# A two-layer attention and expert block: attention normalised in four pieces between pairs of score maxima, its output projection one slot later, and GpSimd's residual sum behind a layer norm

## The reference

```python
x = x + _L0_xattn_ref(_layernorm(x, axis=-1), ctx_768, ...)   # 16 heads of 8
x = x + _L0_ffn_ref(_layernorm(x, axis=-1), ...)              # squared relu; routed part
x = x + _L1_xattn_ref(_layernorm(x, axis=-1), ctx_768, ctx_768, ...)  # one head of 128
x = x + _L1_ffn_ref(_layernorm(x, axis=-1), ...)              # 8 experts, each takes its top tokens
```

```python
attn = jnp.einsum('bhqd,bhkd->bhqk', q, k) * scale
attn = jax.nn.softmax(attn, axis=-1)
x = jnp.einsum('bhqk,bhkd->bqhd', attn, v).reshape(B, Nq, Cq)
return x @ Wo + bo
```

## Time and profile before

| | before |
|---|---|
| median of 3 runs | 264.07 us (263.54 to 264.34) |
| the profiled execution, its own time | 264.77 us |
| its span in the profile | 262.7 us |
| PE busy | 210.8 us, 80% |
| DVE busy | 155.9 us, 59% |
| ACT, POOL busy | 87.5 us (33%), 83.7 us (32%) |
| chain that ended last, by engine | DVE 34%, PE 34%, POOL 11% |
| reciprocals L1260, 5 of them | 13.5 us |
| score maxima L1239, 64 of them | 27.4 us |

### The profile page before, as it was taken

One profiled execution on the slowest core, in us unless ns is written; L12 is line 12 of the kernel. 1 busy time (PEld: TensorE's weight loads), 2 busy tenths in 40 slices (PEclk: granted clock), 3 DMA queues, 4 the chain that ended last, 5 costly groups with the idle time before them and its releaser, 6 DMA issues.

```text
span 262.7 us, 3477 instructions
## 1 busy us (share of the span) xinstructions
PE 210.8 (80%) x1203; PEld 122.6 (47%) x1212; DVE 155.9 (59%) x523; ACT 87.5 (33%) x183; POOL 83.7 (32%) x91
## 2 busy tenths in 40 slices
PE   1797589998799969989999988998897998676400
PEld 0543245335364545366635554653333796666400
DVE  5898837619859989386739665768899122011100
ACT  3241046352433543155402323226710355050200
POOL 1348507000106011101110321300006678885454
PEclk9999999999999999999999999999999999797955
DMA  7600111001100007931100101200001223332222
GB/s 203 176 9 23 45 47 50 20 2 50 30 1 4 0 0 243 331 109 45 41 0 5 40 0 41 85 13 31 0 2 32 53 27 46 43 42 31 24 24 20
DMA packets 15190, 13.04 MB, mean 50 GB/s; under 512 B 3520, under 2 KB 12161, under 8 KB 15169
## 3 DMA queue, kind: packets, MB, share of 16 engines
q1 hardware_dynamic: 11440, 10.17, 12.5%
q0 software_dynamic: 3008, 2.31, 6.5%
q10 hardware_dynamic: 721, 0.30, 0.4%
HBM read 7.99 MB, written 3.21 MB: 43 GB/s over the span
## 4 chain that ended last, share of the span: by engine, by line
DVE 34%; PE 34%; POOL 11%; issue 7%; DMA 6%; ACT 3%; another core or an unknown queue 2%; POOLq 1%; DVEq 0%; ACTq 0%
PE psum L884 7%; POOL out L1632 6%; DVE rden L1260 5%; DVE mrow L1239 5%; DVE xn L1192 4%; PE psum L802 4%; DMA out<-pT,idx 3%; DVE stats L1183 3%; DVE pT L1401 2%; POOL pT L1623 2%; DMA pT<-gather_rows,idx 2%; PE psum L807 2%; PE psum L866 2%; POOL rstd L1563 2%; PE psum L840 2%
## 5 line engine op out<-in xcount | busy, mean ns | idle before, releaser
L802 PE MATMUL psum<-c 128*128 128x512 bf16 x183 | 44.7, 379 | 0.5
L699 ACT ACTIVATE pT<-psum 103x512 f32<-103x512 f32 (+1 forms) x48 | 28.4, 597 | 45.0 <-PE psum L868 44.9
L1562 POOL TENSOR_SCALAR ve<-mv 128x4 f32<-128x4 f32 (+1 forms) x19 | 4.3, 229 | 95.3 <-DVE mv L1186 95.2
L1239 DVE TENSOR_REDUCE mrow<-psum 128x4 bf16<-128x308 f32 x64 | 27.4, 470 | 5.1 <-PE psum L840 4.6
L1632 POOL DMA_INDIRECT out<-pT,idx x16 | 25.4, 1586 | 14.2 <-DMA out<-pT,idx 5.8
L1623 POOL DMA_INDIRECT pT<-gather_rows,idx x16 | 16.7, 1044 | 31.7 <-DVE idx L1461 27.1
L802 PEld LDWEIGHTS psum<-c 128*128 128x128 bf16 x192 | 18.4, 99 | 17.4 <-issue 0.6
L1469 DVE TENSOR_TENSOR pT<-psum,b_rows 128x256 f32<-128x256 f32 x8 | 3.4, 425 | 34.3 <-PE psum L1143 24.1
L840 PE MATMUL psum<-k_stack,q_stack 128*128 128x308 f16 x64 | 16.7, 298 | 7.2 <-DVE mrow L1239 6.8
L773 ACT ACTIVATE pT<-psum,b 128x256 f32<-128x256 f32 x32 | 13.6, 474 | 18.5 <-PE psum L1128 18.5
L1143 PE MATMUL psum<-w,pT 128*128 128x128 f32 x128 | 19.0, 309 | 0.8 <-ACT pT L773 0.8
(11 more groups left out here) (179 smaller groups left out, 352.8 us busy)
## 6 DMA issues: line engine op xcount, KB each, us to landing
w<-in_L_ffn_W SPq DMA_DIRECT2D x16, 256.0 KB, 5.9
gather_rows<-xrow SPq DMA_DIRECT2D x4, 272.0 KB, 2.1
x<-in_x SPq DMA_DIRECT2D x4, 256.0 KB, 4.4
out<-res SPq DMA_DIRECT2D x4, 256.0 KB, 2.0
q_stack<-q_hi SPq DMA_DIRECT2D x24, 32.0 KB, 1.8
q_stack<-q_lo SPq DMA_DIRECT2D x24, 32.0 KB, 1.9
b_rows<-in_L_ffn_b SPq DMA_DIRECT2D x1, 512.0 KB, 3.9
pT<-gather_rows,idx POOLq DMA_INDIRECT x16
```

The costliest lines, as they stand in the source:

```text
L699: nc.scalar.activation(pT[0:n, b % 2, s, :], ST_ps[s % 2][0:n, :], ACT.Exp).then_inc(exp_done, 1)
L802: pe.matmul(bank[b][:, :], ident16, c16[:, 0:4 * P], start=True, stop=True)
L1239: dve.tensor_reduce(mrow[:, b % 2, j, g * GH:(g + 1) * GH], S_ps[u % 2][:, 0:GK].rearrange("p (h k) -> p h k", h=GH), X, ALU.max).then_inc ...
```

## The change

Sequences 0, 1 and 2 are normalised in four quarters of 128 columns, each a reciprocal and a product: two in slot 2, one in slot 4 and one in slot 5 (each behind the score maxima of its slot). The projection on PE and the residual sum on DVE move from slot 5 to slot 6 for these sequences. The last sequence is left as it was. POOL waits, ahead of the residual start and the key stack of sequence 3, until DVE has applied the third layer norm of sequence 0.

```diff
--- before.py
+++ after.py
@@ -974,7 +974,7 @@
                         pe.transpose(tail2_ps[:, 0:E * FC], b1_rows[:], ident[0:E * FC, 0:E * FC]).then_inc(b1_ps_done, 1)
                     for u, j0, j1, ps, _ in units(t) if 0 <= t < B else ():
                         cols = slice(j0 * P, j1 * P)
-                        if s == 5:
+                        if s == (6 if t < B - 1 else 5):
                             pe.wait_ge(attT_done, u + 1)
                             if t == 0:
                                 pe.wait_ge(ld_q, 48)
@@ -1253,12 +1253,14 @@
                                             value_mask[0:CW, c, :].unsqueeze(1).broadcast_to([CW, G, GD]), ALU.mult)
                 ins.then_inc(v8_done, 1)
 
-            def normalise(b):
-                dve.wait_ge(o_ps_done, b + 1)
-                for _, j0, j1, _, _ in units(b):
-                    cols = slice(j0 * P, j1 * P)
-                    settle(dve.reciprocal(rden[:, cols], den_ps[:, cols]))
-                    dve.tensor_tensor(attT[:, cols], O_ps[:, cols], rden[:, cols], ALU.mult).then_inc(attT_done, 1)
+            def normalise(b, j0, j1):
+                if j0 == 0:
+                    dve.wait_ge(o_ps_done, b + 1)
+                cols = slice(j0 * P, j1 * P)
+                settle(dve.reciprocal(rden[:, cols], den_ps[:, cols]))
+                ins = dve.tensor_tensor(attT[:, cols], O_ps[:, cols], rden[:, cols], ALU.mult)
+                if j1 in [end for _, _, end, _, _ in units(b)]:
+                    ins.then_inc(attT_done, 1)
 
             with nc.allow_low_precision("a shift of the exponent that numerator and denominator share"):
                 dve.memset(half_neg[:], -0.5).then_inc(half_set, 1)
@@ -1364,12 +1366,17 @@
                                 settle(dve.tensor_reduce(den1[:, t % 2, js], p1[:, js], X, ALU.add))
                                 dve.reciprocal(r1[:, t % 2, js], den1[:, t % 2, js]).then_inc(r1_done, 1)
                         t = ph - 1
-                        if 0 <= t < B and s == 2:
-                            normalise(t)
+                        if t == B - 1 and s == 2:
+                            for _, j0, j1, _, _ in units(t):
+                                normalise(t, j0, j1)
+                        if 0 <= t < B - 1 and s in (2, 4, 5):
+                            normalise(t, s - 2, s - 1)
+                            if s == 2:
+                                normalise(t, 1, 2)
                         for u, j0, j1, ps, _ in units(t) if 0 <= t < B else ():
                             added = ps[1][:, :].rearrange("p (j d) -> p j d", j=J)[:, j0:j1]
                             stream = rtiles(t)[:, j0:j1]
-                            if s == 5:
+                            if s == (6 if t < B - 1 else 5):
                                 dve.wait_ge(wo_ps_done, u + 1)
                                 dve.wait_ge(res0_done, t + 1)
                                 settle(dve.tensor_tensor(stream, added, stream, ALU.add))
@@ -1599,6 +1606,8 @@
             residual(0)
             for ph in range(B + 2):
                 if ph + 1 < B:
+                    if ph >= 2:
+                        pool.wait_ge(xn_done[2], ph - 1)
                     residual(ph + 1)
                     if ph >= 1:
                         stack_keys(ph + 1)
```

## The result

The changed kernel takes 279.69 us (median of 4 runs, 276.32 to 281.24) against 263.92 for the kernel before (median of 4): ratio 1.0555, 95% interval 1.0457 to 1.0652. The forecast was 272.2 with a range to 275.5. The direction was right and the size too small by almost half. The ratio and its interval compare the means of the fast runs alone (278.6 of three of these four against 263.9), and the run of 281.24 counts as slow.

The account below looks back on a forecast made before the run. DVE's own order was taken to bound phases 1 to 3, with PE waiting. 2.70 + 2.55 + 2.89 = +8.14 on the profiled 264.77 gave 272.9, or 272.2 on the median; range 268.0 to 275.5, own range 270.5 to 274.

Parts of the forecast that it names:

- Bound of the phases: Phases 1 to 3: DVE's own order sets the end, PE waits, and delayed transposes reach the end in full.
- Part 1: Normalisation on DVE: a quarter takes 1.20 us, 0.27 of it fixed; 0.81 more per sequence, 2.4 in all.
- Parts 2 and 3: Maxima between quarters, projection and sum in slot 6: DVE idles; with the pieces' cost, phases +2.70, +2.55, +2.89 us.
- Part 4: POOL's wait around 80 us: applies get 2.9 us back, but only 0.3 reaches the chain, since PE's sums end later.
- rival 3: TensorE's clock falls after PE's waits in slots 6 to 8, once or twice: 273.8 to 275.4 us; chance 0.12.

Follow-up runs that it names:

- the quarters alone: Kernel before with four quarters back to back in slot 2 for sequences 0 to 2, nothing else changed: 266.47 us, ratio 1.0089.
- With the clock held: Changed kernel plus matmuls that nobody reads in PE's waits ahead of the scores of slots 6 and 8, the projection and the transposes: 273.55 us, ratio 1.0355.
- the second trace: Profile of the unmodified changed kernel measured again on one chip beside others: median 279.72 us, ratio 1.0571; the traced execution took 279.61.
- the move alone: Kernel before with only projection and residual sum moved to slot 6 for sequences 0 to 2: 269.34 us, in two groups, ratio 1.0153 for the first.
- all four kernels here: Fillers added to the changed kernel (273.55 us), the projection and sum move (267.74), 384 and 128 column pieces (267.82), and early sequence 0 normalisation with further edits (261.88).

## Why the prediction was wrong

- **Bound of the phases: right.** DVE's order sets them. The idle stretches ahead of the maxima, of L1361 and of the third projection are in the trace with their releasers, within 0.1 us of the forecast; those ahead of the first two residual sums are longer (0.78 and 0.48 for 0.34).
- **Part 1, the pieces: right.** 1.19 a quarter for 1.20 (the reciprocal alone 0.95, where 0.85 was named); the quarters alone cost 2.6 for 2.4.
- **Parts 2 and 3, the order: right in kind, a little small.** With the clock held, the changed kernel is 9.7 above the kernel before, against 8.14. The traces have 0.3 a phase: maxima and `v` take 1.46 when DVE has just idled ahead of them instead of 1.28, the projection to the sum 1.19 (1.49 where the clock fell) instead of 1.16, apply to transposes 1.17 instead of 1.07. I took these steps from rows in which DVE was never idle, where part of each lay beside its neighbour. The last 0.7 of the 9.7 lies outside the phases, which add up to 9.0: the two profiled executions are 8.9 apart (273.63 and 264.77). The prediction took 0.7 off its sum since that execution of the kernel before was so much above its median; the profiled one with PE kept busy is only 0.1 above its own.
- **Part 4, GpSimd's wait: right.** 0.2 us in the trace for 0.3, and no gain that the times can tell.
- **The step that failed is TensorE's clock.** The sum has it at nothing, and rival 3 gave it 0.12 and "1.6 more for a fall", once or twice. Holding the clock gives 6.2 us back (279.7 to 273.6), and the sign that the prediction itself had named, a granted clock below 1.00 between 60 and 130 us, is in both traces of the changed kernel. The chance was too low: it came from one window that had stood it (1.98 us busy of 4), while the change puts such stretches into every phase, and the two traced executions met two and three falls. The price was right only for a short fall: one of 1.6 us is in the second trace too, but others kept the clock low for two to four times as long and cost 3.1, 4.1 and, in the kernel with the move alone, 5.2 us. Rival 3 and the forecast should have been one case.
- How the 15.8 us come about, by runs: quarters 2.6, move 3.7, the clock 6.2. The 3.4 that are left of the 9.7 are a remainder and no run's own measurement: they go with the quarters standing between the maxima, and with whatever quarters and move cost only together.

What stays open: what decides in which of the waits the clock falls, and how long it stays low. In the first trace of the changed kernel a wait of 2.60 us in phase 3 passed without a fall; in the second the clock was down behind it:

```profile
129.43 1.16 PE L982 MATMUL psum<-w_q,attT 128*128 128x128 f32 x8 [2.60 <-DVE attT L1261]
...
135.28 0.66 PE L807 MATMUL psum<-c,xn 128*128 128x128 f32 x4 [0.80 <-DVE xn L1192]
```

## What to carry to other kernels

Where DVE's own order is the path, cutting one of its instructions into pieces to let others in costs the fixed part of each piece, and it pays only if what is let in is ready. Ask for each inserted step when its input comes: here the scores came no sooner, and the steps that used to hide the projection and GpSimd's power had been moved away from beside them. When a change adds waits of TensorE of a microsecond or more to a dense stretch, count the clock into the forecast itself, and test it by filling the waits with matmuls that nobody reads: in all four kernels here that brought the median down, by 1.6 to 6.2 us, and the executions to within 1.8 us of each other.

## What the runs showed of the hardware

- TensorE's granted clock fell to the lower of its levels behind waits close together, the longest of them 1.05 to 2.60 us in the traces, and stayed there for 3 to 14 us (an estimate from the windows' granted clocks), which cost 0.3 to 5.2 us. Ahead of one fall PE was busy for 1.20 us of 4 (the move alone, 68 to 72); in the changed kernel's first trace 1.62 of 4 (92 to 96) and a wait of 2.60 us passed at full clock. Two executions of the same kernel had two falls and three, one of them at the same place.
- DVE's reciprocal from PSUM took 0.95, 1.75, 2.56 and 3.35 us for 128, 256, 384 and 512 columns: 0.8 us for each 128 and 0.15 fixed.
- Four `tensor_scalar` of 128x128 from SBUF to SBUF took 3.9 us beside GpSimd's two `tensor_tensor`, and 1.1 when GpSimd came after them. A reciprocal that reads PSUM took the same beside GpSimd's key stack as without it (128 columns: 0.96 at 85.87, with the key stack running to 86.8, and 0.95 elsewhere).
